# Two edits to a four-stage fp32 kernel: the hand-over from its first stage to its second, and the second stage's output projection in split products

## The chip, the cores and the metric

The kernel runs on one core of a Trainium2 chip. The metric is the device time of one execution in microseconds (us); three executions before the change took 1900.66, 1905.62 and 1904.22 us. Engines are named as in the profile: PE (TensorE matmul), PEld (its weight loads), DVE (VectorE), ACT (ScalarE), POOL (GpSimd), SP (SyncE, whose queue SPq issues the DMAs here).

## The reference, cut to what matters

Two layers, each `x + attention(xn) * silu(ffn(xn))` on `x` of shape (4, 512, 512). The change is in layer 0 alone:

```python
r, k, v, w, g = token-shift mixes of xn, each times its weight      # stage 1
decay = exp(-exp(w))
S = decay * S + k v^T ;  o_t = r_t (S + bonus k v^T)                # 16 heads, scan over 512 steps
o = layernorm_per_head(o) * silu(g)
s = o.reshape(b, t, 256) @ Wo                                       # Wo is 256 x 512, plain fp32 before
gate, up = split(xn @ dequant_fp4(gate_up).T) ; y = (silu(gate) * up) @ dequant_fp4(down).T
x = x + s * silu(y / rms(y))
```

## The kernel before, in words

The program is four blocks, one behind the other: `front`, `recurrence_and_gate`, `linear_attention`, `relu_gate`. Every engine finishes its part of a block before the next block begins. The change touches the first two, and takes one small load out of the third. Each engine's order of work is written out by hand, with a semaphore for each hand-over.

**front** (batches b = 0 to 3) normalises and transposes x, computes r, k, v, w, g, and beside that unpacks a quarter of the FP4 weights per batch. The gate/up weights are unpacked by DVE into `whole` (L415); ACT rounds them to fp32r, the high half (L546); POOL (half jj = 0, L370) or DVE (jj = 1, L435) subtracts to get the low half; both go into `halves`, and SP stores them to a scratch in DRAM, four DMAs of 384 KB per jj (`store_gate_up`, L270). `halves` is one pair of buffers, so jj = 1 may be rounded only when jj = 0 has been stored. In the last batch ACT's order is: v, tanh of the low rank product, decays, r, high half 0, gate tanhs, high half 1; SP's is: store v, w, r, gate/up 0, g, gate/up 1, then the loads that hand over (`relay<-scratch_x`, L328, 1 MB, and `relay<-scratch_v`, L331, 512 KB), then it waits for all stores, and the block ends.

**recurrence_and_gate** starts with SP loading the first gate/up weights (`load_weights(0, 0)`, L865, 1 MB) and waiting for the two handed loads; then ACT and DVE split x into high and low (L1255, L1054), and PE starts. Behind it SP loads keys, values, the next weights, four small constants (`ident` among them) and so on, in one queue. Per batch PE does eleven `gu` jobs (24 passes each, `product3`: three fp32r passes for a product, L694 to L696), four `down` jobs (plain fp32, L1425), and between them: `oT` (8 transposes of the previous batch's gated o, L1342), `s 0` and `s 1` (that batch's output projection, L1353, 4 products of 128x128 by 128x512 each), and `sum n` (the recurrence's outputs, L1397). The order there is gu 3, sum 1, oT, gu 4, s 0, gu 5, sum 2, s 1, gu 6, sum 3. `gu` and its like alternate between two pairs of PSUM banks.

DVE runs 32 units per batch (L1070 and L1074, 1.9 us together) between the `hidden` steps (L1082, L1085) that turn a finished `gu` job into h. `hidden(b, j)` waits for ACT's tanh of `gu j` (L1280). ACT copies the transposed o out of PSUM into `oT` (L1270), which `s 0` waits for. DVE's `attend` (L1160) reads what `s` produced. POOL multiplies each unit's state with r (`read`, L981); `sum n` waits for read 4n + 3. In the first batch `oT` and `s` are skipped. After the last batch the transposes, the copy and both `s` jobs run once more with nothing beside them; then x1 is added and stored, and the block ends.

Of the kernel before, what the change touches and what calls it, by code (L numbers as in the profile page):

```python
# [14 lines left out]
P = 128  # L15
# [105 lines left out]
def front(nc, w, x, spill, wgu, Wdn, relay, hand):  # L121
# [15 lines left out]
    with ExitStack() as ctx:  # L137
# [17 lines left out]
        ident = sb("ident", [P, P])  # L155
# [26 lines left out]
        halves = [sb(f"halves{e}", [P, JQ, 2, 2 * P], F32R) for e in range(2)]  # L182
        g = sb("g", [P, TT, KD])
# [66 lines left out]
        def _(sp):  # L250
# [15 lines left out]
            def store_gate_up(b, jj):  # L266
# [18 lines left out]
            def sequence(b, first=False, last=False):  # L285
# [3 lines left out]
                if not last:  # L289
                    load_x(b + 1)  # L290
                if not first:
# [3 lines left out]
                if last:  # L295
# [5 lines left out]
                    store_gate_up(b, 1)  # L301
# [82 lines left out]
        def _(dve):  # L384
# [47 lines left out]
            def low_gate_up(b):  # L432
# [54 lines left out]
            def sequence(b, first=False, last=False):  # L487
# [18 lines left out]
                if last:  # L506
# [5 lines left out]
                    gates(b + 1)  # L512
                    unpack_down(b, 4, 2)
                    low_gate_up(b)
# [21 lines left out]
        def _(act):  # L536
# [5 lines left out]
            def high_gate_up(b, jj):  # L542
                act.wait_ge(*unpacked.now(b, 3 + jj))
                act.wait_ge(*(gu_stored[0].now(b, 1) if jj > 0 else gu_stored[1].before(b, 1)))
# [37 lines left out]
            def sequence(b, first=False, last=False):  # L582
# [116 lines left out]
def recurrence_and_gate(nc, w, x, spill, wgu, Wdn, x1, relay, parts, handed, hand, retired):  # L699
# [46 lines left out]
    with ExitStack() as ctx:  # L746
# [6 lines left out]
        ident = sb("ident", [P, P])  # L753
        heads = sb("heads", [P, HPT])
        pick = sb("pick", [P, GROUPS_HH, 32])
        Wo = sb("Wo", [P, HH, C])
# [22 lines left out]
        w_part = [sb(f"w_part{i}", [P, 2, KT, 2, P], F32R) for i in range(NW)]  # L779
        tanh_y = sb("tanh_y", [P, 2, C])  # L780
        oT = sb("oT", [P, HH, T])
# [56 lines left out]
        gated_ready = signal("gated_ready", 1)  # L838
        oT_ready = signal("oT_ready", HH)
        sg_ready = signal("sg_ready", TT)  # L840
# [13 lines left out]
        def _(sp):  # L854
# [32 lines left out]
            def body(b, first, last):  # L887
                following = LAST_NEXT_AFTER if last else NEXT_AFTER
                for u in range(AHEAD, AHEAD + UNITS):
# [23 lines left out]
                    if u == 27 and first:  # L913
                        load_gate(0)
                        sp.dma_start(flat(Wo[:, :, :]), w["Wo0"]).then_inc(wo_loaded, 16)
# [11 lines left out]
            load_weights(0, 0)  # L927
            sp.wait_ge(handed, 2 * 16)
# [38 lines left out]
        def _(pool):  # L967
# [35 lines left out]
            def body(b, first, last):  # L1003
                for u in range(AHEAD, UNITS):
                    read(b, u)
                    if u in (14, 17) and not first:
# [33 lines left out]
        def _(dve):  # L1040
            dve.wait_ge(const_set, 3)
            for s in (x_lo_ready, rkb_ready, vc_ready, kv_ready, S_ready, hg_ready, h_ready, o_ready,
                      osum_ready, centred, oss_ready, oveps_ready, yveps_ready, hyr_ready, u1_ready,
                      o_step, gated_ready, sg_ready, o_step, gated_ready, sg_ready):
# [110 lines left out]

            def attend(b, t, place):
# [6 lines left out]
            def finish(b):  # L1163
# [16 lines left out]
                silu(b, 3)  # L1180
                for t in range(TT):
                    attend(b + 1, t, F.place(("s", 0)) if t < 2 else O)

            def body(b, first, last):
# [7 lines left out]
                for j in range(JT):  # L1192
                    hidden(b, j)
                    if j == 0:
                        if first:
                            dve.wait_ge(w_loaded, 4 * 16)
# [50 lines left out]
        def _(act):  # L1247
            for s in (x_hi_ready, vtok_ready, tanh_gate_ready, o_rows_ready, squared, yss_ready, tanh_y_ready,
                      oT_ready, oT_ready):
# [17 lines left out]
            def copy_oT(b, place):  # L1267
                act.wait_ge(*F.product(("oT", 0), b))
                for hh in range(HH):
                    nc.scalar.activation(oT[:, hh, :], place[hh][:, :], ACT.Copy).then_inc(oT_ready.sem, 1)  # L1270
# [24 lines left out]
            def body(b, first, last):  # L1295
                if not first:
                    squares(b - 1, 3)
                    y_tanh(b - 1, 3)
                for j in range(JT):
# [18 lines left out]
                squares(b, 0)  # L1318
                y_tanh(b, 0)
# [14 lines left out]
        def _(pe):  # L1334
# [1098 lines left out]
```

## Time and profile before

| | us |
|---|---|
| three executions | 1900.66, 1905.62, 1904.22 (median 1904.22) |
| the profiled execution | 1898.33, its span 1896.5 |
| PE busy in the span | 1746.1 (92%) |
| DVE, POOL, ACT busy | 1199.6, 578.9, 363.5 |
| front's last matmul ends, the recurrence's first begins | 239.50, 269.46 |
| recurrence, its last matmul record begins | 788.0 |

A row of windows over all engines gives their busy us in the order PE, PEld, DVE, ACT, POOL (and in brackets how many instructions), then PEclk, the DMA engines' busy share and GB/s. A row of the timeline gives the start, the duration, the engine, the line, what was written and read, how many in a row, and in brackets how long the engine had been idle and what released it. PEclk is the TensorE clock that was granted, 1.00 for 2.4 GHz and 0.50 for 1.2 GHz. A PE record is longer than its pace, since records overlap: the pace is the distance between starts. A plain fp32 product shows as two records of one line (64 records at L1353 for 32 products), a split one as one record on each of L694, L695 and L696.

### The profile page before, as it was taken

Reading aid. Unit: us, or ns where it says so; the run is one execution under the profiler, and the core shown is the slowest. Engines: PE = TensorE matmul, PEld = TensorE weight load, DVE = VectorE, ACT = ScalarE, POOL = GpSimd, SP = SyncE. Lnnn points to the kernel's source line nnn. Section 1 sums busy time; section 2 is a strip of 40 time slices with the busy share of each in tenths; the row PEclk is TensorE's granted clock in tenths of the full one; section 3 lists DMA queues with packets and bytes.
Section 4 is the critical chain, followed back from the end, with each engine's and each line's share of the span. In section 5 each row is a group of like instructions: output and inputs, shape, how many; then the busy total and the mean of one; then the engine's idle time right before and its main releaser. Section 6 shows DMA issues by size and latency. Waiting matters only on the chain. (4 is left out here: it accounts for less than half of the span.)

```text
span 1896.5 us, 21740 instructions
## 1 busy us (share of the span) xinstructions
PE 1746.1 (92%) x6900; PEld 1174.6 (62%) x6900; DVE 1199.6 (63%) x1813; ACT 363.5 (19%) x614; POOL 578.9 (31%) x427
## 2 busy tenths in 40 slices
PE   6899927999999999699989999999996899999996
PEld 3444415656566465357757776775774566788885
DVE  6999736778778797347755774784676444423323
ACT  1222210111110211123312221221222111211211
POOL 4668413464455554313301110110111222100001
PEclk9999968999999999899989999999997889999998
DMA  4543376766756755141010010003002111202011
GB/s 183 204 160 125 133 228 226 230 204 204 234 177 205 231 195 191 35 155 40 29 67 1 1 45 22 0 0 111 0 0 67 44 56 59 108 6 83 17 50 33
DMA packets 81307, 197.31 MB, mean 104 GB/s; under 512 B 6352, under 2 KB 28880, under 8 KB 72656
## 3 DMA queue, kind: packets, MB, share of 16 engines
q1 hardware_dynamic: 81232, 196.40, 30.5%
q8 instruction: 35, 0.57, 0.1%
q14 instruction: 40, 0.33, 0.1%
HBM read 152.34 MB, written 44.04 MB: 104 GB/s over the span
## 5 line engine op out<-in xcount | busy, mean ns | idle before, releaser
L981 POOL TENSOR_TENSOR r_rS<-r_S,r_rT 128x512 f32<-128x512 f32 x128 | 184.6, 1445 | 209.3 <-DVE r_S L1074 209.2
L1656 POOL TENSOR_TENSOR l_sq<-l_expq,l_reluq 128x512 f32<-128x512 f32 x64 | 83.0, 1297 | 476.2 <-ACT l_expq L1825 473.4
L694 PE MATMUL r_ps<-relay_part,r_w_part 128*128 128x512 f32 x352 | 148.6, 422 | 47.6 <-DVE relay_part L1054 30.0
L1759 DVE SCALAR_TENSOR_TENSOR l_acc<-l_ps,l_inv,l_acc 128x512 f32<-128x512 f32 x240 | 167.2, 749 | 31.1 <-PE l_ps L696 31.0
L1074 DVE TENSOR_TENSOR_SCAN r_S<-r_dT,r_ps 128x512 f32<-128x512 f32 x128 | 156.4, 1222 | 17.3 <-POOL r_rS L981 13.2
L2152 DVE CAST g_x_part<-g_x 128x512 fp32r<-128x512 f32 x64 | 37.6, 588 | 186.6 <-ACT g_x L2210 186.6
L1425 PE MATMUL r_ps<-Wdn,r_h 128*128 128x512 f32 x352 | 154.6, 595 | 0.0
L695 PE MATMUL r_ps<-relay_part,r_w_part 128*128 128x512 f32 x352 | 141.7, 403 | 0.0
L696 PE MATMUL r_ps<-relay_part,r_w_part 128*128 128x512 f32 x352 | 141.5, 402 | 0.0
L1425 PEld LDWEIGHTS r_ps<-Wdn,r_h 128*128 128x128 f32 x352 | 65.7, 190 | 85.5 <-issue 85.4
L694 PEld LDWEIGHTS r_ps<-relay_part,r_w_part 128*128 128x128 f32 x352 | 68.2, 194 | 76.6 <-issue 45.3
L694 PE MATMUL l_ps<-l_M_part,l_sq_part 128*128 128x512 f32 x256 | 107.9, 421 | 8.0 <-DVE l_sq_part L1774 8.0
L1859 PE MATMUL l_ps<-relay,l_xT 128*128 128x512 f32 x256 | 110.5, 592 | 0.0
L694 PE MATMUL g_ps<-g_x_part,g_Wup 128*128 128x512 f32 x256 | 106.1, 414 | 1.6 <-DVE g_x_part L2140 1.6
L1732 DVE TENSOR_SCALAR l_expq<-l_ps,l_bq 128x512 f32<-128x512 f32 x64 | 48.0, 751 | 93.8 <-ACT l_reluq L1821 93.8
L694 PE MATMUL l_ps<-l_x_part,l_Wq 128*128 128x512 f32 x256 | 105.5, 412 | 0.0
L694 PE MATMUL g_ps<-g_Wdn,g_x_part 128*128 128x512 f32 x256 | 104.8, 410 | 0.0
L695 PE MATMUL g_ps<-g_x_part,g_Wup 128*128 128x512 f32 x256 | 104.2, 407 | 0.0
L696 PE MATMUL g_ps<-g_x_part,g_Wup 128*128 128x512 f32 x256 | 104.0, 406 | 0.0
L696 PE MATMUL l_ps<-l_x_part,l_Wq 128*128 128x512 f32 x256 | 103.9, 406 | 0.0
L695 PE MATMUL l_ps<-l_x_part,l_Wq 128*128 128x512 f32 x256 | 103.4, 404 | 0.0
L695 PE MATMUL l_ps<-l_M_part,l_sq_part 128*128 128x512 f32 x256 | 102.4, 400 | 0.0
(194 smaller groups left out, 3437.5 us busy)
## 6 DMA issues: line engine op xcount, KB each, us to landing
r_w_part<-scratch_wgu SPq DMA_DIRECT2D x44, 1024.0 KB, 6.1
r_V<-scratch_v SPq DMA_DIRECT2D x96, 256.0 KB
scratch_wgu<-f_halves SPq DMA_DIRECT2D x32, 384.0 KB, 4.3
relay<-scratch_x SPq DMA_DIRECT2D x12, 1024.0 KB, 7.1
relay<-scratch_v SPq DMA_DIRECT2D x32, 256.0 KB
relay<-in_x SPq DMA_DIRECT2D x4, 1024.0 KB, 8.3
scratch_x<-f_xT SPq DMA_DIRECT2D x4, 1024.0 KB, 6.9
r_xs<-in_x SPq DMA_DIRECT2D x4, 1024.0 KB, 6.7
```

Source lines behind the costliest of these rows:

```text
L694: nc.tensor.matmul(out, left[1], right[0], start=start, stop=False)
L695: nc.tensor.matmul(out, left[0], right[1], start=False, stop=False)
L696: return nc.tensor.matmul(out, left[0], right[0], start=False, stop=stop)
L981: nc.gpsimd.tensor_tensor(rS[u % RS][:, :], S[u % 2][:, 0:T], rT[u // DK][:, :], ALU.mult).then_inc(rS_ready.sem, 1)
L1074: nc.vector.tensor_tensor_scan(S[u % 2][:, 1:T + 1], dT[hh][:, :], kv, 0.0, ALU.mult, ALU.add).then_inc(S_ready.sem, 1)
L1425: last = nc.tensor.matmul(place[0][:, :], h[:, j, n * P:(n + 1) * P], Wdn[:, j, :], start=(j == 0), stop=(j == JT - 1))
L1656: nc.gpsimd.tensor_tensor(sq[h % 2][:, :], expq[h % 2][:, :], reluq[h % 2][:, :], ALU.add).then_inc(sq_ready.sem, 1)
L1732: nc.vector.tensor_scalar(expq[h % 2][:, :], ring.place(("q", h))[:, :], bq[:, h:h + 1], 0.0, ALU.add, ALU.min).then_inc(minq_ready.sem, 1)
L1759: last = nc.vector.scalar_tensor_tensor(acc[:, t, :], ps, inv[g % 2][:, t:t + 1], acc[:, t, :], ALU.mult, ALU.add)
L1859: last = nc.tensor.matmul(place[:, :], xT[:, kt, n * P:(n + 1) * P], Wkv[kind][:, kt, :], start=(kt == 0), stop=(kt == KT - 1))
L2152: nc.vector.tensor_copy(hi[:, :], x2[j % 2][:, :]).then_inc(x2_hi_ready.sem, 1)
```

## The change: what it does

1. front, last batch: ACT rounds gate/up half 0 ahead of the decays, and half 1 ahead of r, into buffers of their own (`last_halves`, in the memory of `xn` and `mixed_v`), so that half 1 does not wait for the store of half 0. DVE subtracts the low half 1 ahead of the last down unpacking. SP's order of stores stays.
2. The first 1 MB of gate/up weights is loaded into its buffer (`first_part`, now shared by both blocks) by front's SP at the start of the last batch. The recurrence no longer loads it; it waits for three handed loads in place of two.
3. `ident` is loaded once, in front, and not again in the recurrence and in `linear_attention`.
4. The output projection is done as split products: `Wo` is loaded early (at the start of the recurrence's queue, into the buffer of `tanh_y`) and split once, high by ACT at the start of the first batch, low by POOL after `read` 14 of the first batch. o is split per batch: ACT's copy writes the fp32r high half, and DVE subtracts the low half (`low_oT`, two instructions of 128x512), which stands in DVE's order right behind `hidden(b, 4)`. After the last batch it stands behind the last `silu`.

```diff
@@ front, sp: sequence(b, last)
                 if not last:
                     load_x(b + 1)
+                else:
+                    for s in gu_stored:
+                        sp.wait_ge(*s.now(0, 1))
+                    sp.dma_start(first_part[...], wgu[0:P, :]).then_inc(hand, 16)
...
-                    store_gate_up(b, 1)
+                    store_gate_up(b, 1, last_halves)
@@ front, dve
                     gates(b + 1)
+                    low_gate_up(b, last_halves)
                     unpack_down(b, 4, 2)
-                    low_gate_up(b)
@@ front, act
                     low_tanh(b + 1, finally_done, final_place)
+                    high_gate_up(b, 0)
                     decays(b + 1, finally_done, final_place)
+                    gate_tanhs(b + 1)
+                    high_gate_up(b, 1, last_halves)
                     project(b, "r")
-                    high_gate_up(b, 0)
-                    gate_tanhs(b + 1)
-                    high_gate_up(b, 1)
@@ recurrence, sp
-            load_weights(0, 0)
-            sp.wait_ge(handed, 2 * 16)
+            sp.wait_ge(handed, 3 * 16)
+            sp.sem_inc(part_loaded[0].sem, 16)
...
-            sp.dma_start(ident[:, :], w["ident"]).then_inc(w_loaded, 16)
             sp.dma_start(flat(pick[:, :, :]), w["pick"]).then_inc(w_loaded, 16)
             for dst, name in ((heads, "heads"), (bonus, "bonus")):
                 sp.dma_start(dst[:, :], w[name]).then_inc(w_loaded, 16)
+            sp.dma_start(flat(Wo[:, :, :]), w["Wo0"]).then_inc(wo_loaded, 16)
@@ recurrence, pool: body, behind read(b, u)
+                    if u == 14 and first:
+                        pool.wait_ge(Wo_hi_ready, 1)
+                        nc.gpsimd.tensor_tensor(Wo_part[1], Wo, Wo_part[0], ALU.subtract).then_inc(Wo_lo_ready, 1)
@@ recurrence, dve
+            def low_oT(b, place):
+                for hh in range(HH):
+                    dve.wait_ge(*oT_hi_ready.now(b, hh + 1))
+                    nc.vector.tensor_tensor(oT_part[1][:, hh, :], place[hh][:, :], oT_part[0][:, hh, :].bitcast(F32),
+                                            ALU.subtract).then_inc(oT_ready.sem, 1)
...
                 silu(b, 3)
+                low_oT(b + 1, O)
...
                     hidden(b, j)
...
+                    if j == OT_AT + 1 and not first:
+                        low_oT(b, F.place(("oT", 0)))
                     if j == VC_AT:
                         current_value(b)
@@ recurrence, act: body
+                if first:
+                    act.wait_ge(wo_loaded, 16)
+                    nc.scalar.activation(Wo_part[0][:, :, :], Wo[:, :, :], ACT.Copy).then_inc(Wo_hi_ready, 1)
@@ recurrence, pe: project
                     pe.wait_ge(*oT_ready.now(b, HH))
-                    pe.wait_ge(wo_loaded, 16)
+                    pe.wait_ge(Wo_lo_ready, 1)
...
-                        last = nc.tensor.matmul(place[i][:, :], oT[:, hh, t * P:(t + 1) * P], Wo[:, hh, :],
-                                                start=(hh == 0), stop=(hh == HH - 1))
+                        last = product3(nc, place[i][:, :], [q[:, hh, t * P:(t + 1) * P] for q in oT_part],
+                                        [q[:, hh, :] for q in Wo_part], hh == 0, hh == HH - 1)
```

## Rows read from the trace of the kernel before

**Rows 1.** Windows: stretch, its us, engines' busy us, PEclk, DMA share, GB/s.

```profile
254.85:266.30 11.45, 0.00 (x0) 0.00 (x0) 0.00 (x0) 0.01 (x1) 0.21 (x3) 0.50 0.93 308
266.30:307.50 41.20, 24.61 (x104) 18.92 (x104) 25.14 (x30) 5.16 (x9) 12.39 (x9) 0.79 0.87 249
430.00:777.00 347.00, 341.75 (x1323) 207.98 (x1322) 270.00 (x329) 49.53 (x92) 185.31 (x124) 1.00 0.59 196
```

**Rows 2.** Timeline of the seam between front and recurrence.

```profile
229.79 0.60 ACT L560 ACTIVATE f_tlow<-f_ps 128x512 f32<-128x512 f32 x1 [3.08 <-PE f_ps L628]
...
241.67 3.56 POOL L370 TENSOR_TENSOR f_halves<-f_whole,f_halves 128x768 fp32r<-128x768 f32 x2 [15.64 <-ACT f_halves L546]
245.26 2.77 SPq L270 DMA_DIRECT2D scratch_wgu<-f_halves  x4
...
254.85 2.73 SPq L270 DMA_DIRECT2D scratch_wgu<-f_halves  x4
257.63 1.09 SPq L328 DMA_DIRECT2D relay<-scratch_x  x1
258.83 0.97 SPq L331 DMA_DIRECT2D relay<-scratch_v  x1
...
263.06 0.33 SPq L865 DMA_DIRECT2D r_w_part<-scratch_wgu  x1
266.29 2.19 ACT L1255 ACTIVATE relay_part<-relay 128x512 fp32r<-128x512 f32 x4 [13.32 <-SPq L929]
...
269.46 0.76 PE L694 MATMUL r_ps<-relay_part,r_w_part 128*128 128x512 f32 x1 [29.96 <-DVE relay_part L1054]
```

**Rows 3.** Timeline, DVE in front's last batch, an unpacking step.

```profile
220.89 5.55 DVE L394 TENSOR_SCALAR f_shifted<-f_gu_words,f_shift 128x768 uint32<-128x768 uint32 x1
```

**Rows 4.** Timeline, PE at job gu 3 of the first batch.

```profile
307.59 0.76 PE L694 MATMUL r_ps<-relay_part,r_w_part 128*128 128x512 f32 x1 [5.66 <-DMA r_w_part<-scratch_wgu]
```

**Rows 5.** Timeline, first batch: POOL's read 15 and PE's sum 3.

```profile
339.42 1.67 POOL L981 TENSOR_TENSOR r_rS<-r_S,r_rT 128x512 f32<-128x512 f32 x1 [0.19 <-DVE r_S L1074]
...
341.47 0.16 PEld L1397 LDWEIGHTS r_ps<-r_rS,r_pick 128*32 128x32 f32 x8 [0.37 <-POOL r_rS L981]
```

**Rows 6.** Timeline, batch 1: s 0, what DVE does then, s 1.

```profile
443.82 3.59 PE L1353 MATMUL r_ps<-r_Wo,r_oT 128*128 128x512 f32 x8
...
446.05 1.21 DVE L1091 TENSOR_TENSOR r_vc<-r_v_tok,r_ps 128x1024 f32<-128x1024 f32 x1
...
454.18 3.70 PE L1353 MATMUL r_ps<-r_Wo,r_oT 128*128 128x512 f32 x8 [0.19 <-DVE r_u L1160]
```

**Rows 7.** Timeline: successive records of split products, and of plain fp32 ones.

```profile
275.06 0.39 PE L694 MATMUL r_ps<-relay_part,r_w_part 128*128 128x512 f32 x1
275.29 0.39 PE L695 MATMUL r_ps<-relay_part,r_w_part 128*128 128x512 f32 x1
...
444.68 0.19 PEld L1353 LDWEIGHTS r_ps<-r_Wo,r_oT 128*128 128x128 f32 x1 [0.24 <-issue]
...
445.11 0.19 PEld L1353 LDWEIGHTS r_ps<-r_Wo,r_oT 128*128 128x128 f32 x1 [0.24 <-issue]
```

**Rows 8.** Windows of PE alone: stretch, its us, PE busy, PEclk, DMA share, GB/s.

```profile
292.00:294.00 2.00, 0.00 (x0) 1.00 0.78 231
294.00:296.00 2.00, 1.62 (x7) 1.00 1.06 303
...
308.00:310.00 2.00, 2.00 (x6) 0.50 0.55 208
...
782.00:784.00 2.00, 2.00 (x4) 0.50 0.00 0
```

**Rows 9.** Timeline after the last batch: the copy of oT, the projection's start and end.

```profile
778.62 1.07 ACT L1270 ACTIVATE r_oT<-r_ps 128x512 f32<-128x512 f32 x2
...
779.79 0.67 PE L1353 MATMUL r_ps<-r_Wo,r_oT 128*128 128x512 f32 x1 [2.66 <-DVE r_u L1153]
...
788.63 1.41 DVE L1160 SCALAR_TENSOR_TENSOR r_u<-r_ps,r_hyr,r_u 128x512 f32<-128x512 f32 x2 [2.02 <-PE r_ps L1353]
```

More of the change, by code:

```diff
@@ L118, in tiled, with front @@
     return wgu.rearrange("(j p) (h k n) -> p j h k n", p=P, h=2, k=KT)
-def front(nc, w, x, spill, wgu, Wdn, relay, hand):
+def front(nc, w, x, spill, wgu, Wdn, relay, ident, first_part, hand):
     MIX = ["r", "w", "k", "v", "g"]
@@ L154, in front @@
         bg = sb("bg", [P, KD])
-        ident = sb("ident", [P, P])
         x_tok, delta = relay[0:2]
@@ L182, in front @@
         halves = [sb(f"halves{e}", [P, JQ, 2, 2 * P], F32R) for e in range(2)]
+        last_halves = [flat(buffer[:, :, :])[:, 0:JQ * 4 * P].bitcast(F32R).rearrange("p (j h n) -> p j h n", j=JQ, h=2)
+                       for buffer in (xn, mixed_v)]
         g = sb("g", [P, TT, KD])
@@ L290, in sequence @@
                     load_x(b + 1)
+                else:
+                    for s in gu_stored:
+                        sp.wait_ge(*s.now(0, 1))
+                    sp.dma_start(first_part[:, :, :, :, :].bitcast(F32).rearrange("p h k s n -> p (h k s n)"),
+                                 wgu[0:P, :]).then_inc(hand, 16)
                 if not first:
@@ L540, in _, with high_gate_up @@
                 s.ahead(act)
-            def high_gate_up(b, jj):
+            def high_gate_up(b, jj, halves=halves):
                 act.wait_ge(*unpacked.now(b, 3 + jj))
-                act.wait_ge(*(gu_stored[0].now(b, 1) if jj > 0 else gu_stored[1].before(b, 1)))
+                if halves is not last_halves:
+                    act.wait_ge(*(gu_stored[0].now(b, 1) if jj > 0 else gu_stored[1].before(b, 1)))
                 for e in range(2):
@@ L696, in product3, with recurrence_and_gate @@
     return nc.tensor.matmul(out, left[0], right[0], start=False, stop=stop)
-def recurrence_and_gate(nc, w, x, spill, wgu, Wdn, x1, relay, parts, handed, hand, retired):
+def recurrence_and_gate(nc, w, x, spill, wgu, Wdn, x1, relay, parts, ident, first_part, handed, hand, retired):
     UNITS = HH * DK
@@ L751, in signal @@
             return Signal(ctx, nc, "r_" + name, per, unit)
-        ident = sb("ident", [P, P])
         heads = sb("heads", [P, HPT])
         pick = sb("pick", [P, GROUPS_HH, 32])
-        Wo = sb("Wo", [P, HH, C])
+        Wo_part = [sb(f"Wo_part{i}", [P, HH, C], F32R) for i in range(2)]
         bonus = sb("bonus", [P, HH])
@@ L776, in recurrence_and_gate @@
         small = {s: sb(s, [P, TT * NH]) for s in ("osum", "oss", "oveps", "orstd")}
-        w_part = [sb(f"w_part{i}", [P, 2, KT, 2, P], F32R) for i in range(NW)]
+        w_part = [first_part] + [sb(f"w_part{i}", [P, 2, KT, 2, P], F32R) for i in range(1, NW)]
         tanh_y = sb("tanh_y", [P, 2, C])
-        oT = sb("oT", [P, HH, T])
+        Wo = tanh_y
+        oT_part = [sb(f"oT_part{i}", [P, HH, T], F32R) for i in range(2)]
         u1 = [sb(f"u1{t}", [P, C])[:, :] for t in range(TT)]
@@ L1269, in copy_oT @@
                 for hh in range(HH):
-                    nc.scalar.activation(oT[:, hh, :], place[hh][:, :], ACT.Copy).then_inc(oT_ready.sem, 1)
+                    nc.scalar.activation(oT_part[0][:, hh, :], place[hh][:, :], ACT.Copy).then_inc(oT_hi_ready.sem, 1)
             def square_o(b):
@@ L1318, in body @@
                 squares(b, 0)
+                if first:
+                    act.wait_ge(Wo_lo_ready, 1)
                 y_tanh(b, 0)
@@ L1452, in _, with linear_attention @@
                 counted = F.index[job] + 1
-def linear_attention(nc, w, x1, spill, relay, handed, hand):
+def linear_attention(nc, w, x1, spill, relay, ident, handed, hand):
     AHEAD = 2
@@ L1586, in _ @@
             sp.sem_inc(x_loaded.sem, 16)
-            sp.dma_start(ident[:, :], w["ident"]).then_inc(ident_loaded, 16)
             for dst, name in ((bkv["k"], "bk"), (bkv["v"], "bv"), (bq, "bq")):
@@ L2406, in build, with stages @@
         relay = [outer.enter_context(nc.sbuf_tensor(f"relay{i}", shape, F32)) for i in range(3)]
+        ident = outer.enter_context(nc.sbuf_tensor("ident", [P, P], F32))
         handed = [outer.enter_context(nc.semaphore(f"handed{i}")) for i in range(3)]
-        stages(nc, w, out, spill, x1, relay, parts, handed)
-def stages(nc, w, out, spill, x1, relay, parts, handed):
+        stages(nc, w, out, spill, x1, relay, parts, ident, handed)
+def stages(nc, w, out, spill, x1, relay, parts, ident, handed):
     with ExitStack() as ctx:
@@ L2414, in stages @@
         Wdn = ctx.enter_context(nc.sbuf_tensor("Wdn", [P, B * DQ, C], F32))
-        retired = front(nc, w, w["x"], spill, wgu, Wdn, relay, handed[0])
-        recurrence_and_gate(nc, w, w["x"], spill, wgu, Wdn, x1, relay, parts, *handed[0:2], retired)
-    linear_attention(nc, w, x1, spill, relay, *handed[1:3])
+        first_part = ctx.enter_context(nc.sbuf_tensor("first_part", [P, 2, KT, 2, P], F32R))
+        retired = front(nc, w, w["x"], spill, wgu, Wdn, relay, ident, first_part, handed[0])
+        recurrence_and_gate(nc, w, w["x"], spill, wgu, Wdn, x1, relay, parts, ident, first_part, *handed[0:2], retired)
+    linear_attention(nc, w, x1, spill, relay, ident, *handed[1:3])
     relu_gate(nc, w, x1, spill, out, relay, parts, handed[2])
```

23 lines of the change are left out of this document (12 added, 11 removed).

## The prediction

> **What bounds the kernel now.** I read the windows first. From 430 to 777 us, which is batches 1 to 3 of the recurrence, PE is busy 341.75 of 347 us at a granted clock of 1.00, DVE 270 us, the DMA engines 0.59 [rows 1]: PE bounds this stretch, so a matmul saved there is time saved, and whatever PE is made to wait is time lost. The seam before it is another matter. From 254.85 to 266.3 us no engine works and DMA moves 308 GB/s; up to 307.5 us PE has 24.6 of 41.2 us and DMA still moves 249 GB/s at a share of 0.87 [rows 1]. That is a stretch bound by transfers.
>
> The timeline of the seam shows the chain [rows 2]. PE ends at 239.5 (269.46 less 29.96). POOL subtracts half 0 until 245.23, SP stores it, the second half is stored only from 254.85, both hand-over loads queue behind it (257.63, 258.83), ACT starts at 266.29 when they have landed, and PE at 269.46. With x split 1.35 us after ACT's start, PE could have begun at 267.7: the rest is the first weights, issued at 263.06.
>
> **Part 1, the seam.** In the new order ACT rounds half 0 right behind the tanh that begins at 229.79 [rows 2]: 230.4 to 232.0. POOL's two subtractions (3.56 us [rows 2]) run until 235.6. DVE's next unpacking step is of the kind that once took 5.55 us while POOL was at work [rows 3], so I let it wait for POOL; the 3.5 us of unpacking behind it end at 239.1, ACT's second rounding (1.6 us) at 240.8, and ACT's two copies of r (1.2 us) at 242.0. SP stores r ahead of half 0, so its burst begins at 242.05, with everything else ready by then. Were DVE not held, it would be 240.5.
>
> From there the DMA engines decide. r 0.52 MB, half 0 1.57, g 0.52, half 1 1.57, x 1.05, v 0.52 make 5.77 MB. At the 308 GB/s of the old burst [rows 1] that is 18.7 us, and as that rate contains one start-up I take 17.7: the loads land at 259.8. Old landing: 266.2. The gain is 6.4 us. Bounds: by SP's issues alone v goes out at 250.0 and, with its old 7.4 us (258.83 to 266.2 [rows 2]), lands at 257.4, a gain of 8.8; at 308 GB/s with a start-up on top it is 261.9, a gain of 4.3.
>
> PE's own start would move from 269.46 to about 261.2, 8.3 us, since the first weights have long arrived. But PE waits again for weights, 5.66 us before gu 3 at 307.59 [rows 4], behind a queue of transfers at a share of 0.87 [rows 1]. So the landing there counts, not PE's start. The queue has lost the rest of the first weights (some 0.7 MB after 266.3) and ident, has gained Wo (0.26 MB), and now begins with an empty pipe for 2 us or so, where before the first weights filled it. I call this even: 6.4 us carry through. If the queue shrinks by the whole 0.7 MB, 2.5 us more; if Wo alone tells, 1 us less. The load moved into front runs beside compute (DMA share there is small) and I cost it at nothing; ACT's split of Wo (1.1 us) precedes a tanh whose reader on DVE comes some 15 us later, also nothing. Without ident, linear_attention saves nothing: its first transposes wait for the normalisation.
>
> **Part 2a, splitting Wo.** POOL subtracts 128x1024 behind read 14. By its 1.78 us for 128x768 [rows 2] that is 2.4 us. Read 15 could start at 339.42 and sum 3 already follows POOL (341.47, released by it [rows 5]). With 1.67 us cut to 1.3 for want of DVE beside it, read 15 ends at 343.1 in place of 341.1: PE loses 1.8 us, once. Nothing absorbs it. Bounds 1.2 and 2.4.
>
> **Part 2b, the products.** A plain product is two records 0.43 apart, 0.857 us; a split pass takes 0.233 (275.06 to 275.29), three take 0.70 [rows 7]. Each product saves 0.159 us, the 24 in the loop 3.8 us, the 8 at the end 1.3 us. The Trainium skill ("FP8 and Floating Point Precision", "TensorE Precision Notes") counts true fp32 as four passes; four against three at equal cost would save 0.214 us each, 6.8 us over 32, and the sum below would be 1.7 us lower. The rows differ: a split pass costs 0.233, not a quarter of 0.857, and I keep the rows.
>
> **Part 2c, the wait that it adds.** Here is the price. s 0 began at 443.82, right behind gu 4, because oT had been copied 5 us earlier [rows 6]. Now it waits for `low_oT`, which DVE holds behind `hidden(b, 4)`, and that waits for gu 4 itself, ACT's tanh and two DVE steps. Those steps let the next DVE instruction start at 446.05 [rows 6]. Two subtractions of 0.69 us there end at 447.43, PE goes on at 447.5: 3.68 us of a standing PE, with gu 5, sum 2 and s 1 queued behind it. The shorter s 0 and s 1 return 1.27 us and the 0.19 us that s 1 waited for `attend` [rows 6] goes: attend, 1.4 us later, still comes before s 1. Net 2.2 us per batch, 6.7 us for batches 1 to 3. DVE is 1.4 us later from here, and late for nothing, PE being later still. Bounds 2.0 and 2.9 (if PE's later waits took none of it back and s 1 saved nothing).
>
> **Part 2d, the clock.** A standing PE can lose its clock. After the 5.66 us before 307.59 [rows 4] the window from 308 is at 0.50; after the 2.66 us before the last projection [rows 9] that from 782 is at 0.50; but at 292 to 294, with no matmul at all, and behind it, it stayed at 1.00 [rows 8]. So stops near 3 us go either way, and 3.5 us is beyond the one that was spared. The price of a fall: the last projection takes 8.84 us (779.79 to 788.63 [rows 9]) where 16 records at 0.43 are 6.86, so 2.0 us; for split passes, somewhat less bound by the array, 1.8. I take three falls, 5.4 us; bounds 0 and 6. The Trainium skill ("TensorE: Matmul & The Clock Gate", "HAM oscillation — how this bites in real kernels") warns of just this, a stop inside a loop that makes each next group start cold. By it all three fall, and the sum is the one below; by the spared window it could be 5.4 us less. The rows cannot settle it.
>
> **Part 2e, the end.** DVE's subtractions follow the copy (778.62 + 1.07 [rows 9]); the second ends at 780.8 in place of 779.69, PE starts 1.1 us later. Its 24 passes take 5.6 us and a fall 1.8: 7.4 against 8.84. Net -0.3.
>
> **Sum.** -6.4 + 1.8 + 6.7 + 5.4 - 0.3 = +7.2 us. The profiled execution took 1898.33 us (span 1896.5), so 1905.5 by its measure. It lies 5.9 us under the median of the three executions, 1904.22, and I add the change to that: 1911.4, say 1911.
>
> **Rivals.**
> - *The clock holds in the loop.* For it the window at 292 [rows 8], against it the two falls. The sum is then +1.8, 1906: no change that can be told.
> - *The seam gives all that it looks like.* If the transfers run as SP can issue them and the shorter queue brings gu 3's weights 2.5 us sooner still, -11.3 in place of -6.4. Against it stand 308 and 249 GB/s at shares of 0.93 and 0.87 [rows 1]. With falling clocks +2.3, 1906.5; no change.
> - *Faster: the wait before gu 3 closes.* One mechanism, in the transfers between 266 and 307 us. It decides if the weights of gu 3 land more than 13 us sooner (8.8 from the landing, and 4 or more out of the 5.66 us that PE now waits [rows 4], because the prefetched megabyte no longer stands in the queue). The seam is then -13 to -14.5; with a clock that falls at most once, -4 to -7, about 1898.
> - *Slower still: the burst jams.* The stores and loads of the seam mix, and the hand-over lands only 2 us sooner: +11.6, 1916.
> - *The split does not pay.* If fp32r passes with these operands ran at the plain pace of 0.43 for two, nothing of 5.1 us is saved: 1916 also. The split gu passes at 0.233 speak against it.
>
> **Chances and range.** Forecast 0.47 (its own range 1907 to 1915); the clock holds 0.17; the full seam 0.12; faster 0.13; the two slow ones 0.11. About 0.3% (5.7 us) is what a measurement of this kernel can tell from no change. Of the forecast some 0.10 falls within it. So: faster 0.13, within 0.3% 0.39, slower 0.48. The range of 8 in 10 leaves out the far end on both sides and allows 3 us for the executions' own spread: 1899 to 1919.
>
> **What would show it.** Right: L1255 starts near 260 and PE near 261; in batches 1 to 3 PE stands some 3.5 us before s 0, released by the new DVE subtraction, the window behind it at 0.50; sum 3 of the first batch about 2 us behind POOL; L694 to L696 with oT and Wo at 0.233. Wrong: s 0 behind gu 4 without a stop, a clock of 1.00 in all three, or gu 3 of the first batch earlier by over 10 us.

## The result, and the profile after

| | median us | runs | against the kernel before |
|---|---|---|---|
| before | 1902.44 | 4 (1895.75 to 1905.62) | |
| changed | 1925.96 | 4 (1920.09 to 1929.12) | 1.0135, 95% interval 1.0108 to 1.0163 |

The change made the kernel slower, by 1.35%. Forecast were 1911 us and a range that ended at 1919: right in its sign, wrong in its size by some 15 us. The profiled execution took 1928.31 us (span 1926.5), 30.0 us more than that of before.

Where those 30 us come from can be read off the timelines of PE, at points that both kernels pass:

| PE, us | before | after | after less before |
|---|---|---|---|
| front's last matmul ends | 239.50 | 240.56 | +1.1 |
| the recurrence's first begins | 269.46 | 263.37 | -6.1 |
| gu 3 of the first batch begins | 307.59 | 303.38 | -4.2 |
| the recurrence's first transposes of o begin (batch 1) | 436.9 | 433.5 | -3.4 |
| its last transposes of o begin | 776.1 | 785.2 | +9.1 |
| its last matmul ends | 788.60 | 798.36 | +9.8 |
| the last matmul of linear_attention ends | 1447.61 | 1476.01 | +28.4 |
| the last matmul ends | 1882.16 | 1911.90 | +29.7 |

Up to 798 us the sum of the prediction (+7.2) stands within 3 us of what happened. Two thirds of the loss arise behind it, in linear_attention, of which the change touches one small load.

**The seam.** Timeline after, as for [rows 2] (start, duration, engine, line, tiles, in brackets the idle time before and its releaser):

```profile
240.19 0.84 ACT L553 ACTIVATE f_xn<-f_whole 128x768 fp32r<-128x768 f32 x1 [3.57 <-DVE f_whole L421]
...
242.77 0.33 SPq L276 DMA_DIRECT2D scratch_r<-f_outr  x1
...
252.75 1.12 SPq L334 DMA_DIRECT2D relay<-scratch_x  x1
253.97 0.97 SPq L337 DMA_DIRECT2D relay<-scratch_v  x1
...
261.87 2.19 ACT L1277 ACTIVATE relay_part<-relay 128x512 fp32r<-128x512 f32 x4 [19.13 <-SPq L938]
...
263.37 0.76 PE L701 MATMUL r_ps<-relay_part,first_part 128*128 128x512 f32 x1 [22.81 <-DVE relay_part L1067]
```

The second rounding began at 240.19 (its end was forecast for 240.8) and r was stored at 242.77 (forecast 242.05). ACT began on the handed loads at 261.87, where 259.8 was forecast for their landing: 4.4 us sooner than the 266.29 of before.

**Sum 3 and Wo, first batch**, against [rows 4, 5]:

```profile
303.38 0.77 PE L701 MATMUL r_ps<-relay_part,first_part 128*128 128x512 f32 x1 [3.78 <-DMA first_part<-scratch_wgu]
```

```profile
334.22 2.39 POOL L1017 TENSOR_TENSOR r_Wo_part<-r_tanh_y,r_Wo_part 128x1024 fp32r<-128x1024 f32 x1
336.57 1.71 POOL L990 TENSOR_TENSOR r_rS<-r_S,r_rT 128x512 f32<-128x512 f32 x1
```

```profile
338.33 1.07 PE L1424 MATMUL r_ps<-r_rS,r_pick 128*32 128x512 f32 x8 [1.88 <-POOL r_rS L990]
```

POOL's subtraction took 2.39 us (2.4 forecast), read 15 moved behind it and took 1.71 us (1.3 forecast), and PE stood 1.88 us (1.8 forecast).

**The wait before s 0**, batch 1, against [rows 6]:

```profile
442.11 0.69 DVE L1098 SCALAR_TENSOR_TENSOR r_h<-r_hg,r_ps 128x512 f32<-128x512 f32 x1
442.71 1.28 DVE L1172 TENSOR_TENSOR r_oT_part<-r_ps,r_oT_part 128x512 fp32r<-128x512 f32 x2
```

```profile
444.10 0.72 PE L701 MATMUL r_ps<-r_Wo_part,r_oT_part 128*128 128x512 f32 x1 [3.45 <-DVE r_oT_part L1172]
444.61 0.63 PE L702 MATMUL r_ps<-r_Wo_part,r_oT_part 128*128 128x512 f32 x1
445.04 0.63 PE L703 MATMUL r_ps<-r_Wo_part,r_oT_part 128*128 128x512 f32 x1
...
448.06 0.40 PE L702 MATMUL r_ps<-r_Wo_part,r_oT_part 128*128 128x512 f32 x1
448.29 0.39 PE L703 MATMUL r_ps<-r_Wo_part,r_oT_part 128*128 128x512 f32 x1
```

PE stands 3.45 us (3.68 forecast), and again 3.46 and 3.37 us in batches 2 and 3. Behind the stop the passes come 0.43 us apart, at 448 us 0.23: the clock fell and came back. The windows (stretch, its us, PE busy, PEclk, DMA share, GB/s) say the same:

```profile
444.00:446.00 2.00, 1.90 (x5) 0.54 0.71 270
446.00:448.00 2.00, 2.00 (x7) 0.61 0.33 84
570.00:572.00 2.00, 1.85 (x5) 0.61 0.72 290
699.00:701.00 2.00, 1.80 (x6) 0.79 0.73 297
```

**linear_attention.** The waits of PE between 800 and 1480 us (engine, line, releaser: us in total, times, longest) have one group that the kernel before has not:

```profile
PE l_ps L1874 <- issue: 12.3, 4, 4.0
```

"Issue" is time in which the engine waited for nothing that the profile shows. The four stops lie at two places, the two turns of this stage's loop, which lead into its third and its fourth batch. The two at the first turn, in the timeline:

```profile
1140.52 0.39 PE L703 MATMUL l_ps<-l_M_part,l_sq_part 128*128 128x512 f32 x1
1143.54 1.08 PE L1874 MATMUL l_ps<-ident,relay 128*128 128x128 f32 x5 [2.63 <-issue]
1148.06 2.18 PE L1874 MATMUL l_ps<-ident,relay 128*128 128x128 f32 x9 [3.44 <-issue]
```

Before, the same transposes followed their matmul with nothing between:

```profile
1129.99 0.39 PE L696 MATMUL l_ps<-l_M_part,l_sq_part 128*128 128x512 f32 x1
1130.22 1.91 PE L1851 MATMUL l_ps<-l_ident,relay 128*128 128x128 f32 x16
```

The clock fell behind the stops. Windows of PE behind the first turn, first before, then after:

```profile
1132.00:1134.00 2.00, 2.00 (x7) 1.00 0.96 393
```

```profile
1150.00:1152.00 2.00, 2.00 (x6) 0.50 0.00 0
```

What PE waited for is told by another row, that of a DMA queue which brings instructions (packets, MB, share of 16 engines). First before, then after:

```profile
q8 instruction: 35, 0.57, 0.1%
```

```profile
q8 instruction: 53, 0.87, 0.2%
```

The 18 more are packets of 16 KB. By the packets' times in the trace none came between 1105.4 and 1469.2 us before the change. After it nine came from 1139.0 to 1278.4 us and nine from 1306.5 to 1446.0 us, in the two iterations that follow a turn; those at 1139.0 and 1139.7 us lie right before the first of the two stops shown, that at 1145.8 us within the second. The reading is that before the change the loop's code stayed in the engine, and that after it the code was fetched again on each turn. The loop is the same in both, 1572 PE instructions, but it has moved: counted in the built program it lay at instructions 5512 to 7084 of PE before, and lies at 5560 to 7132 now. Each matmul record and each weight load counts as one instruction, so a plain fp32 product is four and a split one six, and the eight products of the projection make 16 more in each of the three copies of the batch, 48 in all.

The Trainium skill ("Runtime: NRT & Kernel Launch", "Instruction fetch mechanics") says that instructions come in blocks of 16 KB, which are 256 instructions, fetched ahead in sequence, and that a taken branch to a block which is no longer held stalls for the fetch. The packets of 16 KB and the stops at the taken branch agree. In such blocks, counted from the program's first PE instruction, the loop's end moved from 0.67 of its block to 0.86.

### The profile page after: what moved, and what is told of

It is laid out like the page before. It is cut to its first block and busy times, and to the rows that moved or that the text cites. A ratio compares the mean times of both kernels' runs of the same rounds, so it can differ in the third digit from the quotient of the medians.

```text
span 1926.5 us, 21819 instructions
## 1 busy us (share of the span) xinstructions
PE 1756.1 (91%) x6932; PEld 1191.3 (62%) x6932; DVE 1209.4 (63%) x1821; ACT 364.8 (19%) x615; POOL 580.5 (30%) x428
## 5 line engine op out<-in xcount | busy, mean ns | idle before, releaser
L1783 DVE SCALAR_TENSOR_TENSOR l_acc<-l_ps,l_inv,l_acc 128x512 f32<-128x512 f32 x240 | 166.9, 749 | 28.4 <-PE l_ps L703 28.2
L1882 PE MATMUL l_ps<-relay,l_xT 128*128 128x512 f32 x256 | 114.6, 609 | 0.0
L701 PE MATMUL g_ps<-g_Wdn,g_x_part 128*128 128x512 f32 x256 | 105.0, 410 | 0.0
L701 PE MATMUL r_ps<-relay_part,r_w_part 128*128 128x512 f32 x224 | 93.2, 416 | 10.6 <-DVE r_h L1098 7.8
L703 PE MATMUL g_ps<-g_Wdn,g_x_part 128*128 128x512 f32 x256 | 102.3, 400 | 0.0
L702 PE MATMUL g_ps<-g_Wdn,g_x_part 128*128 128x512 f32 x256 | 101.9, 398 | 0.0
L2106 POOL TENSOR_TENSOR g_xs<-g_xs,relay 128x512 f32<-128x512 f32 x16 | 21.6, 1349 | 264.5 <-DVE relay L2156 252.2
```

The source lines that it names most:

```text
L701: nc.tensor.matmul(out, left[1], right[0], start=start, stop=False)
L702: nc.tensor.matmul(out, left[0], right[1], start=False, stop=False)
L703: return nc.tensor.matmul(out, left[0], right[0], start=False, stop=stop)
L1783: last = nc.vector.scalar_tensor_tensor(acc[:, t, :], ps, inv[g % 2][:, t:t + 1], acc[:, t, :], ALU.mult, ALU.add)
L1882: last = nc.tensor.matmul(place[:, :], xT[:, kt, n * P:(n + 1) * P], Wkv[kind][:, kt, :], start=(kt == 0), stop=(kt == KT - 1))
L2106: nc.gpsimd.tensor_tensor(xs[:, t % 2, :], xs[:, t % 2, :], s[:, t, :], ALU.add).then_inc(out_ready.sem, 1)
```

## The experiments

Theory F: the loss in linear_attention is the price of where its loop lies in PE's code. Rivals: the shared ident, or the chance of the clock. For the rest the theory is the prediction's own: seam, Wo, stop before s 0, clock. Kernels were moved in PE's code by `pe.sem_inc(pad, 1)`, n times, a semaphore that nobody waits for. They ran in three groups of four; a group shares its chip and its runs of before (medians 1900.48, 1897.91 and 1898.74 us), and 0.1% of the time is 1.9 us. An interval is some 4 us to either side, so differences between two kernels are good to 5 or so.

### 1 to 4: code moved alone, and the seam alone

```diff
@@ 1: before.py, linear_attention, tensor
+            for _ in range(47):
+                pe.sem_inc(pad, 1)
@@ 2 and 3: the changed kernel, same place, 209 and 81
@@ 4: the changed kernel, projection as before
-                        last = product3(nc, place[i][:, :], [q[...] for q in oT_part], [q[...] for q in Wo_part], ...)
+                        last = nc.tensor.matmul(place[i][:, :], oT[:, hh, t * P:(t + 1) * P], Wo[:, hh, :], ...)
```

> The kernel before with 47 semaphore increments added on PE at the start of linear_attention, nothing else. In the change the split projection adds 48 PE instructions ahead of that block (positions counted in the built program: the loop of linear_attention lies at 5512 to 7084 before, 5560 to 7132 after). Theory F (the loop's body moved against the instruction buffer, and is fetched anew each time round): +14 to +20 us against the kernel before, waits named issue ahead of the transposes at the two loop turns (near 1135 and 1295 us) of some 12 us in all, the clock at 0.50 behind them, more fetches of 16 KB. Rival (the loss in linear_attention comes from the shared ident, the relay or a chance of the clock): 0 to +2 us, since none of these is in this kernel.

> The changed kernel with 209 semaphore increments on PE at the start of linear_attention: its loop then lies 257 instructions (one block of 16 KB and one instruction) behind where it lay before the change. Theory F: the issue waits at the two loop turns are gone, batches 2 and 3 of linear_attention take 156 to 159 us each as before; -14 to -20 us against the changed kernel, so +4 to +9 us against the kernel before (1907 to 1912 us), which is the change's own sum of the prediction. Rival: the waits stay, 1926 to 1932 us.

> The changed kernel with 81 semaphore increments in the same place: the loop then lies at 5641 to 7213, that is half a block (129 instructions) behind its old place. Two forms of theory F: (a) what counts is where in its block the loop's last instruction lies (before: 0.67 of a block, no refetch; after: 0.86, refetch; here 0.18): then no refetch, about as e2, 1905 to 1911 us. (b) Any place but the old one in the block is bad, or the block count is what counts: the waits stay, 1925 us or more. The rival to F: 1925 us or more.

> The changed kernel with the projection in plain fp32 as before, Wo loaded at its old place, so the seam, first_part and the shared ident alone. PE's instructions lie as before the change. Theory F and the prediction's part 1: -4 to -7 us against the kernel before (1896 to 1899 us), batches of linear_attention as before. If the shared ident or the relay were the cause of the loss in linear_attention: +10 us or more. If the seam's gain is given back later: within 2 us of before.

| | median us | ratio, 95% | loop's end in its block | packets | issue waits at the turns |
|---|---|---|---|---|---|
| 1 before + 47 | 1917.54 | 1.0098 (1.0059 to 1.0137) | 0.86 | 53 | 12.0 us |
| 2 changed + 209 | 1929.37 | 1.0158 (1.0124 to 1.0192) | 0.68 | 36 | none |
| 3 changed + 81 | 1911.42 | 1.0065 (1.0042 to 1.0088) | 0.18 | 35 | none |
| 4 seam alone | 1892.28 | 0.9962 (0.9940 to 0.9984) | 0.67 | 35 | none |

The first settles it. The kernel before, with no line of the change in it, shows the change's stops and its 53 packets once its code is moved by 47 instructions, and it is 18.6 us slower (11.2 to 26.0) than before in the same group. Of these 3.1 are the increments' own (the wait for the stage's first transposes is 15.4 us, not 12.3). Waits of PE between 1100 and 1430 us:

```profile
PE l_ps L1854 <- issue: 12.0, 4, 3.7
```

The second and third take the stops away again, but the second's time was missed: 1929 us, not 1907 to 1912. The third, at 1911.4, came just above its 1905 to 1911. The waits show why. I had costed the increments at nothing, and they stand ahead of the stage's first transposes. That wait was 12.4 us; with 209 and with 81 it is

```profile
PE l_ps L1877 <- issue: 38.4, 1, 38.4
```

```profile
PE l_ps L1877 <- issue: 18.7, 1, 18.7
```

128 increments more cost 19.7 us, 0.154 each, and by that some 40 fit under the old wait. Less these 26.0 and 6.3 us both kernels are, by the ratios, 4 to 6 us above before, where the prediction's sum has +7.2. The third also says that the old place is not the only good one.

The fourth shows the seam alone: -7.2 us (-3 to -11). It shares ident and has neither stops nor more packets, which rules out that rival. The same work runs once more as the eleventh below, and stands there at -1.1 us (-4.9 to +2.7).

### 5 to 8: the increments under a wait, and the prediction's steps undone one by one

```diff
@@ 5 to 7: the changed kernel, recurrence_and_gate, tensor, under the wait for the hand-over
+            for _ in range(81):
+                pe.sem_inc(pad, 1)
@@ 6 and 7, dve: low_oT ahead of hidden(b, 4)
-                    if j == OT_AT + 1 and not first:
-                        low_oT(b, F.place(("oT", 0)))
...
                         for u in range(following[j], following[j + 1]):
                             unit(b, u)
+                    if j == OT_AT and not first:
+                        low_oT(b, F.place(("oT", 0)))
@@ 7, pool
-                    if u == 14 and first:
+                    if u == 16 and first:
@@ 8: kernel 4, with 49 increments there
```

> The changed kernel with 81 semaphore increments on PE at the start of recurrence_and_gate, where PE stands some 23 us for the hand-over: the loop of linear_attention lies at 5641 to 7213 as in the run with 81 in linear_attention, but the increments lie under a wait (there they cost 6.3 us ahead of the first transposes: 18.7 us in place of 12.4). Theory F: no issue waits at the loop turns, and 5 to 7 us less than that run: +5 to +10 us against the kernel before (1906 to 1911). If it is 1920 us or more, the increments themselves, not their place in code, had changed something.

> As the kernel with 81 increments in the seam, and low_oT stands ahead of hidden(b, 4), where DVE waits 2.93 us for ACT anyway (438.46 to 441.39 in the trace of the changed kernel). Theory of the prediction's steps 2c and 2d: the three PE stops before s 0 (3.45, 3.46, 3.37 us) go, and the clock's falls behind them: 3 x (3.4 + 1.8) = 15.6 us less than the kernel with the seam's increments alone, bounds 10 (the clock falls anyway) and 18. Rival (the stop is only moved, since PE waits for DVE's later steps instead): 3 us less or none.

> As the kernel with the early low_oT, and POOL subtracts Wo's low half behind read 16 in place of read 14, so that sum 3 does not wait for it. Prediction's step 2a: 1.9 us less than the kernel with early low_oT alone (the stop at 336.46 goes), bounds 0 (sum 4 waits in its place) and 3. Against the seam alone (-8 us against before) it should be 4 to 6 us faster by the cheaper products (step 2b: 3.8 + 1.3 us): 12 to 14 us under the kernel before. Rival (the products save nothing): equal to the seam alone.

> The seam alone (plain fp32 projection; -8 us against before) with 49 semaphore increments on PE in the seam, which lie under its wait: the loop of linear_attention then lies at 5561 to 7133, one instruction off its place in the changed kernel. Theory F's price by itself: four issue waits of 12.3 us in all and 3 to 8 us of clock behind them, +15 to +20 us against the seam alone, so +7 to +12 against before. Rival (the waits need the split projection): -8 us as the seam alone.

| | median us | ratio, 95% | packets | first to last transposes of o |
|---|---|---|---|---|
| 5 changed, code moved | 1906.54 | 1.0043 (1.0024 to 1.0061) | 35 | 351.7 us |
| 6 and low_oT early | 1897.99 | 0.9997 (0.9977 to 1.0017) | 35 | 339.2 us |
| 7 and Wo behind read 16 | 1891.71 | 0.9964 (0.9944 to 0.9983) | 35 | 337.7 us |
| 8 seam alone, code moved | 1907.46 | 1.0051 (1.0031 to 1.0071) | 53 | 340.0 us |

The last column is the loop of the recurrence; it is 339.2 us in the kernel before, 351.7 in the changed one, 338.6 with the seam alone.

The fifth is the change without its effect on linear_attention: +8.2 us (+4.6 to +11.6), where the prediction's sum was +7.2. Some 2 us of it are its increments in the seam: gu 3 begins at 305.36, against 303.38 in the changed kernel.

In the sixth the stop before s 0 is gone, and the loop is 12.5 us shorter. Two rows, the loop's windows of PE, say what that is made of (first the fifth, then the sixth):

```profile
435.44:787.17 351.73, 335.89 (x1309) 0.98 0.57 190
```

```profile
436.36:775.61 339.25, 330.81 (x1308) 0.99 0.60 197
```

PE's waits fell by 7.3 us: the three stops of 10.3 us went, and 2.8 us came in their place, for `attend` ahead of s 1. PE's busy time fell by 5.1 us with the same matmuls in the loop, and that is the clock. The median fell by 8.6 us, less than the 10 that I had put as the lower bound. In the seventh's trace DVE subtracts while it would wait for ACT, and PE goes from gu 4 into s 0 without a gap:

```profile
439.13 1.26 DVE L1173 TENSOR_TENSOR r_oT_part<-r_ps,r_oT_part 128x512 fp32r<-128x512 f32 x2
442.14 0.69 DVE L1096 SCALAR_TENSOR_TENSOR r_hg<-r_tanh_gate,r_ps 128x512 f32<-128x512 f32 x1 [1.75 <-ACT r_tanh_gate L1303]
```

```profile
441.01 0.39 PE L703 MATMUL r_ps<-relay_part,r_w_part 128*128 128x512 f32 x1
441.24 0.39 PE L701 MATMUL r_ps<-r_Wo_part,r_oT_part 128*128 128x512 f32 x1
```

The seventh also takes away the stop before sum 3, and is 6.3 us faster by the medians. The stop alone is 1.9 us, and from the recurrence's first matmul to the first transposes of o of batch 1 the traces have 2.7 us; the rest of the 6.3 no single row accounts for. Behind the stop, in the sixth, the clock fell, which in the changed kernel it had not done; in the seventh the same stretch has neither (windows of PE, first of the sixth, then of the seventh):

```profile
337.00:339.00 2.00, 0.78 (x8) 1.00 0.90 271
339.00:341.00 2.00, 2.00 (x9) 0.61 1.05 263
341.00:343.00 2.00, 2.00 (x7) 0.54 0.60 187
```

```profile
337.00:339.00 2.00, 2.00 (x10) 1.00 0.52 196
339.00:341.00 2.00, 2.00 (x13) 1.00 0.68 195
341.00:343.00 2.00, 2.00 (x11) 1.00 0.95 401
```

But the seventh, at 0.9964, is no faster than the seam alone at 0.9962, where 4 to 6 us less were expected. The loop's windows (first the seam alone, then the seventh) show that the products are cheaper, by 3.7 us of PE's busy time, both at a clock of 1.00, and the loop only 0.9 us shorter:

```profile
427.87:766.43 338.56, 333.07 (x1285) 1.00 0.59 197
```

```profile
434.27:771.94 337.67, 329.37 (x1308) 1.00 0.60 198
```

The waits of PE say where the rest went, without the one ahead of the last projection. First the seam alone (between 424 and 771 us), then the seventh (430 to 777):

```profile
PE r_ps L701 <- DVE r_h L1090: 2.2, 3, 1.8
PE r_ps L701 <- DVE r_u L1158: 1.8, 2, 0.9
PE r_ps L1402 <- POOL r_rS L986: 1.0, 4, 0.3
PE r_ps L1358 <- DVE r_u L1165: 0.3, 2, 0.2
```

```profile
PE r_ps L701 <- DVE r_h L1099: 2.2, 3, 1.8
PE r_ps L701 <- DVE r_u L1167: 1.8, 2, 1.0
PE r_ps L701 <- DVE r_u L1180: 1.8, 3, 0.8
PE r_ps L1427 <- POOL r_rS L991: 1.5, 4, 0.5
PE r_ps L701 <- DVE r_oT_part L1173: 0.9, 1, 0.9
```

PE waits 2.9 us more: for `attend` ahead of s 1 (L1180, the bank of s 0), for low_oT once, for POOL. 3.7 less 2.9 is the 0.9 us, but for rounding. Behind the loop the split takes it back: the wait ahead of the last projection is 3.6 us (2.7 with the seam alone), and that projection runs 8.4 us (7.1). The increments in the seam cost something too, ahead of the loop: the first matmul of the recurrence starts at 270.52 and gu 3 at 305.30, against 263.12 and 301.80 with the seam alone.

The eighth has the seam's code and the change's place in memory: the stops are back (12.4 us in four), and it is 16.9 us above the seam alone by the ratios, across two groups.

### 9 to 12: where the border lies, and whether the split can be made to pay

```diff
@@ 9: kernel 7, but 40 increments in linear_attention in place of the 81
@@ 10: 9, and 41 increments at the start of front
@@ 11: kernel 4, 24 increments in linear_attention
@@ 12: kernel 10, and
-    VC_AT = 4
+    VC_AT = 5
```

> Seam, split projection, early low_oT and Wo behind read 16, with 40 semaphore increments at the start of linear_attention alone, the fewest that bring the loop's last instruction into the next block: it lies at 5600 to 7172, its end at 0.02 of block 28, its start still in block 21. They cost nothing there (of the first transposes' 12.4 us some 6 are free; a single increment costs 0.154 us by the two runs with 209 and 81). If the place of the end within its block decides (theory F, form a): no issue waits, and 3 to 5 us less than the kernel of the same edits with 81 increments in the seam (1891.7), as those cost 3.5 us by gu 3 of the first batch: 1887 to 1890 us. If the number of blocks that the loop touches decides (8 here, 7 in all kernels without the waits and in those with them): the waits return, 1903 us or more.

> The same edits, with 40 increments in linear_attention and 41 at the start of front, where PE stands 12.2 us for the first x: the loop at 5641 to 7213, known to be free of the waits, at no cost on the path. By theory F 3 to 5 us less than the kernel with 81 in the seam: 1886 to 1890 us, -9 to -12 against before and 2 to 5 under the seam alone. Rival (the split projection gives nothing beside the seam, as its saving turns into waits for DVE): equal to the seam alone, -7 us against before.

> The seam alone, with 24 increments at the start of linear_attention (under the wait for the first transposes), which halve the shift: the loop at 5536 to 7108, its end at 0.77 of block 27. Between 0.67 (no waits) and 0.86 (waits) this looks for the border. With the border above 0.77: -7 us against before, as the seam alone. Below it: +9 us. Nothing in the runs so far favours one; I take the border at three quarters of the block and expect the waits, 0.6 to 0.4.

> As the kernel with 41 and 40 increments, and DVE's current_value (1.2 us) stands behind hidden(b, 5) in place of hidden(b, 4), so that attend of the first half comes 1.2 us sooner. In the kernels with early low_oT the split projection saves 3.8 us of PE in the loop, but PE waits 1.6 to 2.3 us more ahead of s 1 for DVE's attend. Theory (the saving turns into that wait): the wait before s 1 goes in two or three batches, -1.5 us in the trace from the transposes of batch 0 to the last ones (337.6 us in the kernel with 81 in the seam, 338.5 with the seam alone), total -1 to -2 us. Rival (it is taken back by gu 6 or 7, which need the banks that attend of the second half frees): 0.

| | median us | ratio, 95% | loop's end in its block | packets |
|---|---|---|---|---|
| 9 | 1893.09 | 0.9983 (0.9960 to 1.0005) | 0.02 | 35 |
| 10 | 1891.56 | 0.9978 (0.9958 to 0.9998) | 0.18 | 35 |
| 11 | 1896.34 | 0.9994 (0.9974 to 1.0014) | 0.77 | 35 |
| 12 | 1892.92 | 0.9981 (0.9963 to 0.9999) | 0.18 | 35 |

The ninth touches eight blocks and has no stops, so the count of blocks alone does not decide. In the eleventh I took the border to lie at three quarters of the block, and missed: at 0.77 the loop stays in. All three kernels with the loop's end at 0.86 have the stops, all of 0.67, 0.68, 0.77, 0.02 and 0.18 have none. So a stretch of bad places begins between 0.77 and 0.86 of a block and, if it is one stretch, ends before 0.02 of the next, some 64 instructions at most. What sets it is open; the loop's start moves with its end in every run, so it could as well be the start's place.

The eleventh is the work of the fourth with increments that lie under a wait, and is 4 us slower by its median (6 by the ratios), in another group of runs and on another chip. No wait accounts for that; so a difference of 5 us between kernels of different groups proves nothing. The ninth to twelfth did not reach the 1886 to 1890 us that I expected.

Whether the split brings anything on top of the seam is therefore open. Across groups the seventh and the fourth are equal. Within the last group, which shares a chip, the ninth, tenth and twelfth (all split) lie 3.3, 4.8 and 3.4 us under the eleventh (the seam alone) by their medians, where each interval is some 4 us to either side. From the first transposes of o of batch 1 to the recurrence's last matmul the traces have 350.7 us for the split in the seventh and tenth, and 349.4, 352.5 and 352.4 for plain fp32 in the fourth, eighth and eleventh. The plain kernels differ more among themselves than from the split ones.

In the twelfth the wait before s 1 went from 1.8 to 0.2 us, and the loop is no shorter (338.6 us, 337.7 in the tenth). Waits for POOL's reads came in its place, 3.7 us where the tenth has 1.5, and PE was busy 1.3 us longer at a clock of 0.99. I had expected banks, and it is this row (345 to 760 us):

```profile
PE r_ps L1427 <- POOL r_rS L993: 3.7, 4, 1.6
```

## Why the prediction was wrong, step by step

- **"Without ident, linear_attention saves nothing", and no term for the stages behind the recurrence.** This is the step that failed: about ident it was right, but nothing else was asked of the stages behind. The change was counted in engine time, and the 48 instructions that it adds to PE's code were not counted at all. They move a loop of another stage to a place where its code is fetched anew on each turn; the kernel before, moved by 47 instructions, has the same stops. Price by the traces: from the recurrence's last matmul to the last of linear_attention it is 659.0 us before, 661.7, 661.0, 661.8 and 661.0 in kernels 4 to 7, but 677.7 in the changed kernel, 675.0 in the eighth and 673.1 in the first (less 3.1 for its increments). That is 12 to 17 us above kernels 4 to 7, of which 12.0 to 12.4 are stops; the clock, at 0.50 behind them, is the likely rest. By the ratios it is 17 us (changed less fifth, and eighth less fourth, each across two groups).
- **Part 1, the seam: -6.4.** Landing and start were 2 us later than forecast (4.4 us gained, at the lower bound of 4.3, which had a start-up on top of the 308 GB/s; no row showed the 1 us that the forecast took off for it). By gu 3 it was -4.2, or -5.3 without the later end of front; alone, in the whole time, -7.2 (-3 to -11) in one group and -1.1 (-4.9 to +2.7) in another. The sign of the step stands, its size is not known better than that.
- **Part 2a, Wo: +1.8.** 1.88 measured.
- **Parts 2b, 2c and 2d in the loop: the products, the stop and the clock, +12.1 together.** From the first to the last transposes of o it was +12.5 us (351.7 against 339.2), and the parts stand too. The stops before s 0 are 10.3 us (11.0 forecast). The products are 3.7 us of busy time, by the seventh against the fourth (3.8 forecast). The clock is 5.1 us by the fifth less the sixth, and 5.6 by the changed kernel's busy time in the loop (335.86, against 333.99 before) with the 3.7 put back; 5.4 were forecast, though no row had shown the 1.8 us of a fall for split passes. All three stops cost the clock, so the rival in which it holds is out.
- **What part 2b did not say.** The cheaper products count in full only while PE stands at the stop. Without the stops PE waits 2.9 us more for DVE and POOL.
- **Part 2e, the end: -0.3.** The trace has +0.7 (785.2 to 798.36 against 776.1 to 788.60): PE stood 3.6 us in place of 2.66, and its 24 passes took 8.5 us where 7.4 were forecast, at a clock of 0.50 from 790 to 792.
- **The sum.** +7.2 forecast for all but the failed step; +8.2 (+4.6 to +11.6) measured in the fifth kernel, some 6 without its increments. In the loop each part came near its forecast. That the totals meet as well is in part luck, since the seam's size is not known to better than some 4 us.

## What to carry to other kernels

A change also has a length. Count the instructions that it adds to each engine's stream; if a long loop lies behind it, look at the packets of the instruction queue and at waits named "issue" at the loop's turn, in stages that the change does not touch too. Before such a loss is put down to the change itself, move the unchanged kernel's code by as much: one run tells. And take an edit that saves PE time only with the waits that follow it: here 3.7 us of cheaper products were 0.9 us of shorter loop, and a subtraction placed one step earlier in DVE's order shortened it by 12.5.

## What the runs showed of the hardware that was not expected

- A loop of 1572 PE instructions can stay in the engine over its turns, or not, by its place alone: 35 packets of instructions against 53, no stops against four of 12.0 to 12.4 us in all. Moving it by 47 instructions is enough, and 40 beyond the changed kernel's place repair it.
- The Trainium skill, in the section named above, also speaks of a window of two blocks for taken branches, though it gives PE a larger instruction memory than most engines, of 2048 instructions. For PE this case's traces differ from the window: a loop of 1572 instructions, 6.1 blocks long, turned without a stop and without fetching its code again in 11 kernels of 14, and with both in three. The measurement decides.
- A semaphore increment by PE cost 0.154 us when nothing hid it (38.4 less 18.7 us over 128), but between 47 and 81 of them one cost 0.10 (15.4 and 18.7 us).
- A stop of 1.9 us was followed by a clock of 0.61 and 0.54 in one kernel (the sixth, at 338 us) and by 1.00 in another (the changed one, at 338 us). The same stop of 2.66 us ahead of the last projection was followed by 0.50 in the kernel before (782 to 784 us) and by 1.00 in the seam alone (772 to 774 us), and its 16 records took 8.84 and 7.10 us. The executions of one kernel differ by some 10 us either way, and the slowest has a lower mean clock than the fastest in all twelve experiments (1880.06 us at 0.961 and 1898.31 at 0.954 in the fourth): where the clock falls is part of that.
